# A table for the order of three PSUM banks, and a quarter of one product moved from GpSimd to VectorE

## What is computed

```
dA  = exp(dt[..., None] * A)                       # 256 inner channels x 16 states
dBx = dt[..., None] * B_t[:, None, :] * x_t[..., None]
h   = dA * h + dBx                                 # along the sequence
y   = einsum('bdn,bn->bd', h, C_t)
```

## Time and profile before

| | us |
|---|---|
| median of 3 runs (14129.7 to 14130.83) | 14129.91 |
| the profiled execution | 14134.33 |
| its span, first to last instruction | 14132.5 |

### The profile page before, as it was taken

How to read it: one execution, slowest core, us unless ns; L and a number is a source line. 1 busy time by engine, 2 the same in 40 slices (tenths; PEclk the granted TensorE clock), 3 DMA queues, 4 the chain that set the end, 5 groups by cost and what they waited for, 6 DMA issues and landing times.

```text
span 14132.5 us, 159372 instructions
## 1 busy us (share of the span) xinstructions
PE 11209.6 (79%) x32512; PEld 3280.3 (23%) x32512; DVE 13252.0 (94%) x11827; ACT 12050.3 (85%) x24489; POOL 13788.4 (98%) x3076
## 2 busy tenths in 40 slices
PE   6787777777787878778777778787787878887787
PEld 2222222222222222222222222222222222222221
DVE  7999999999999999999999999999999999999998
ACT  7888888888888888888888888888888888888887
POOL 7999999999999999999999999999999999999999
PEclk8888888888888888888888888888888888888887
DMA  5656565555656565656566565656565665656564
GB/s 131 143 137 143 140 149 138 143 137 145 143 142 145 135 146 140 146 138 142 139 147 144 139 145 136 149 139 143 140 141 142 145 144 137 143 140 149 138 143 113
DMA packets 1068201, 1991.56 MB, mean 141 GB/s; under 512 B 123650, under 2 KB 124731, under 8 KB 1067067
## 3 DMA queue, kind: packets, MB, share of 16 engines
q1 hardware_dynamic: 1065786, 1979.41, 58.8%
q10 hardware_dynamic: 1280, 0.02, 0.0%
HBM read 1626.62 MB, written 352.32 MB: 140 GB/s over the span
## 4 chain that ended last, share of the span: by engine, by line
POOL 66%; issue 31%; DVE 1%; ACT 1%; PE 1%; POOLq 0%; ACTq 0%; DMA 0%; DVEq 0%; SPq 0%
POOL hq L953 50%; POOL dbx L945 16%; DVE hq L844 0%; POOLq L952 0%; ACTq L496 0%; PE pp L378 0%; ACT ps_a L584 0%; PE pp L355 0%; POOLq L944 0%; ACT L544 0%; PE pp L356 0%; PE pp L319 0%; DVE dbx L830 0%; ACT xh L544 0%; POOLq L942 0%
## 5 line engine op out<-in xcount | busy, mean ns | idle before, releaser
L844 DVE TENSOR_TENSOR_SCAN hq<-ps_a,dbx 128x512 f32<-128x512 f32 x8192 | 9507.5, 1208 | 700.1 <-ACT dbx L595 461.5
L953 POOL TENSOR_TENSOR hq<-hq,c_rep 128x2048 f32<-128x2048 f32 x2048 | 9255.2, 4546 | 231.8 <-ACT carry L600 231.3
L584 ACT ACTIVATE ps_a<-dt_rep,A_neg 128x512 f32<-128x512 f32 x8192 | 5621.4, 687 | 1508.4 <-DVE hq L844 1477.7
L945 POOL TENSOR_TENSOR dbx<-dtx_rep,b_rep 128x2048 f32<-128x2048 f32 x1024 | 4646.5, 4538 | 90.9 <-DMA dtx_rep<-dtx_d 90.9
L411 PE MATMUL ps_acc<-hq,dsum 128*32 128x512 f32 x16384 | 2470.3, 679 | 485.8 <-POOL hq L953 482.5
L595 ACT ACTIVATE dbx<-ps_a,dbx,carry 128x1 f32<-128x1 f32 x7168 | 2510.9, 350 | 252.5 <-POOL dbx L945 150.7
L830 DVE TENSOR_TENSOR dbx<-dtx_rep,ps_b 128x2048 f32<-128x2048 f32 x1024 | 2316.7, 2262 | 4.8 <-DMA dtx_rep<-dtx_d 4.8
L319 PE MATMUL pp<-xin,diag 128*128 128x504 f32 (+3 forms) x4608 | 2213.2, 608 | 6.0 <-ACT diag L626 6.0
L399 PE MATMUL ps_b<-dbl,bsel 41*128 41x512 f32 x2048 | 1320.9, 729 | 276.4 <-issue 223.2
L355 PE MATMUL pp<-x,W_taps 128*128 128x512 f32 x768 | 687.2, 993 | 750.1 <-DVE x L804 606.7
L319 PEld LDWEIGHTS pp<-xin,diag 128*128 128x128 f32 x4608 | 792.9, 189 | 1397.9 <-issue 1397.9
(11 more groups left out here) (117 smaller groups left out, 9982.4 us busy)
## 6 DMA issues: line engine op xcount, KB each, us to landing
dtx_rep<-dtx_d SPq DMA_DIRECT2D x2048, 256.0 KB, 4.9
dt_rep<-dt_d SPq DMA_DIRECT2D x2048, 256.0 KB, 5.7
c_rep<-bc_d SPq DMA_DIRECT2D x1024, 256.0 KB, 5.5
b_rep<-bc_d SPq DMA_DIRECT2D x1024, 128.0 KB, 2.9
dtx_d<-sp SPq DMA_DIRECT2D x256, 512.0 KB, 2.8
dt_d<-dt SPq DMA_DIRECT2D x256, 512.0 KB, 6.1
out<-o SPq DMA_DIRECT2D x128, 512.0 KB, 5.2
xin<-in_x SPq DMA_DIRECT2D x192, 320.0 KB, 8.5
```

What stands on the lines that cost most here:

```text
L584: A(ps_a[:, i % RA, :], dt_rep[:, q // NQ, g, :], ACT.Exp, scale=A_neg[:, q // NQ, q % NQ, g:g + 1]).then_inc(exp_done, 1)
L844: v.tensor_tensor_scan(hq[:, q % HQ, g, :], ps_a[:, i % RA, :], dbx[:, slot(q), g, :], 0.0, ALU.mult, ALU.add).then_inc(scan_done, 1)
L945: g.tensor_tensor(dbx[:, slot(q), :, :], dtx_rep[:, d, :, :], b_rep[:, c % 2, q % NQ // 2, :].unsqueeze(1).to_broadcast([P, DG, T]), ALU.m ...
L953: g.tensor_tensor(quad, quad, c_rep[:, c % 2, q % NQ, :].unsqueeze(1).to_broadcast([P, DG, T]), ALU.mult).then_inc(cmul_done, 1)
```

## The change

The bank of a tile comes from a table `BANK`, and the distance to the tile that had it before from `AGE`. The distance is 3, but 2 for tiles 15 and 31, and 4 for the tiles behind them, 16 and the next chunk's 0. Decay, add_carry and scan read the table. Tile 0 of the product of quad 3 (of 4 tiles) is made by VectorE behind the scan of tile 7; GpSimd makes the other three tiles. TensorE selects B for it in slot 6. So `ps_b` is used five times a chunk rather than four, the semaphore `bmul_dve` counts five products, and whoever reads quad 3 waits for both engines.

```diff
--- before.py
+++ after.py
@@ -67,10 +67,16 @@
     return u // 8, 2 * (u % 2) + i % 2, (u % 8) // 2
 
 
-def bank_age(i):
-
-    return RA if i >= RA else next(NT + i - j for j in range(NT - 1, 0, -1) if j % RA == i % RA)
-
+HURRIED = (15, 31)
+BANK = [0, 1, 2]
+for tile in range(3, NT):
+    BANK.append(BANK[tile - (2 if tile in HURRIED else 4 if tile - 1 in HURRIED else 3)])
+AGE = [2 if tile in HURRIED else 4 if (tile - 1) % NT in HURRIED else 3 for tile in range(NT)]
+assert all(BANK[tile] == BANK[tile - AGE[tile]] for tile in range(NT))
+
+BY_DVE = (0, 2, 3, 4, 6)
+ND, SHARED, SPLIT = len(BY_DVE), 3, 1
+PE_SHARED, DVE_SHARED = 6, 7
 
 POOL_CHUNKS, POOL_SLOTS, ATT_CHUNK = (1, 2, 3, 4), (10, 11), CH - 3
 ATT_FC, ATT_H, ATT_MM, ATT_SUM, ATT_EXP, ATT_WTS = 24, 25, 26, 28, 29, 31
@@ -249,7 +255,7 @@
                     sp_e.wait_ge(dtx_out, 16 * (b * CH + c + 1))
                     sp_e.sem_inc(wait_taken, 1)
                 if not (isinstance(b, int) and b * CH + c == 0):
-                    sp_e.wait_ge(bmul_dve, (b * CH + c - 1) * (QUADS // 2) + 2 * (d + 1))
+                    sp_e.wait_ge(bmul_dve, (b * CH + c - 1) * ND + sum(q // NQ <= d for q in BY_DVE))
                     sp_e.sem_inc(wait_taken, 1)
                     sp_e.wait_ge(bmul_pool, (b * CH + c - 1) * (QUADS // 2) + 2 * (d + 1))
                     sp_e.sem_inc(wait_taken, 1)
@@ -392,7 +398,7 @@
                 mm(pp[:, 1, 0:2], w["gblock"][:], gst[:], start=True, stop=True).then_inc(gmm_done, 1)
 
             def select_b(b, c, q):
-                n = (b * CH + c) * (QUADS // 2) + q // 2
+                n = (b * CH + c) * ND + BY_DVE.index(q)
                 pe.wait_ge(dbl_done, b * CH + c + 1)
                 if not (isinstance(n, int) and n == 0):
                     pe.wait_ge(bmul_dve, n)
@@ -420,6 +426,8 @@
                             select_b(b, c, s + 2)
                         elif c + 1 < end:
                             select_b(b, c + 1, 0)
+                    if u == PE_SHARED:
+                        select_b(b, c, SHARED)
                     if c + 1 < end:
                         for d in range(DI):
                             if u == PE_XH[d]:
@@ -547,7 +555,7 @@
                 act.wait_ge(dbl_mm, b * CH + c + 1)
                 if not (isinstance(b, int) and b * CH + c < 2):
                     act.wait_ge(bc_out, 16 * (b * CH + c - 1))
-                    act.wait_ge(bsel_mm, (b * CH + c - 1) * (QUADS // 2))
+                    act.wait_ge(bsel_mm, (b * CH + c - 1) * ND)
                 A(dbl[0:NDBL, c % 2, :], pp[0:NDBL, 0, :], ACT.Copy).then_inc(dbl_done, 1)
 
             def softplus_tail(b, c, k):
@@ -580,19 +588,22 @@
                 if i % (DG * NQ) == 0:
                     act.wait_ge(dt_repd[q // NQ], 16 * NJ * (b * CH + c + 1))
                 if not (isinstance(n, int) and n < RA):
-                    act.wait_ge(scan_done, n - bank_age(i) + 1)
-                A(ps_a[:, i % RA, :], dt_rep[:, q // NQ, g, :], ACT.Exp,
+                    act.wait_ge(scan_done, n - AGE[i] + 1)
+                A(ps_a[:, BANK[i], :], dt_rep[:, q // NQ, g, :], ACT.Exp,
                   scale=A_neg[:, q // NQ, q % NQ, g:g + 1]).then_inc(exp_done, 1)
 
             def add_carry(b, c, i):
                 q, g = divmod(i, DG)
                 m = (b * CH + c) * QUADS + q
                 if g == 0:
-                    act.wait_ge(bmul_pool if q % 2 else bmul_dve, (b * CH + c) * (QUADS // 2) + q // 2 + 1)
+                    if q % 2:
+                        act.wait_ge(bmul_pool, (b * CH + c) * (QUADS // 2) + q // 2 + 1)
+                    if q in BY_DVE:
+                        act.wait_ge(bmul_dve, (b * CH + c) * ND + BY_DVE.index(q) + 1)
                     act.wait_ge(carry_done, m - QUADS + 1)
                 act.wait_ge(exp_done, (b * CH + c) * NT + i + 1)
                 first = dbx[:, slot(q), g, 0:1]
-                A(first, ps_a[:, i % RA, 0:1], ACT.Identity, scale=carry[:, q, g:g + 1], bias=first).then_inc(first_done, 1)
+                A(first, ps_a[:, BANK[i], 0:1], ACT.Identity, scale=carry[:, q, g:g + 1], bias=first).then_inc(first_done, 1)
 
             def keep_carry(b, c, q):
                 n = (b * CH + c) * QUADS + q
@@ -821,27 +832,33 @@
 
             def weigh_inputs(b, c, q):
                 d = q // NQ
-                dve.wait_ge(bsel_mm, (b * CH + c) * (QUADS // 2) + q // 2 + 1)
+                dve.wait_ge(bsel_mm, (b * CH + c) * ND + BY_DVE.index(q) + 1)
                 if q % NQ == 0:
                     dve.wait_ge(dtx_repd[d], 16 * NJ * (b * CH + c + 1))
                 n = (b * CH + c) * QUADS + q
-                if not (isinstance(n, int) and n < 2):
-                    dve.wait_ge(scan_done, DG * (n - 1))
-                v.tensor_tensor(dbx[:, slot(q), :, :], dtx_rep[:, d, :, :],
-                                ps_b[:].unsqueeze(1).to_broadcast([P, DG, T]), ALU.mult).then_inc(bmul_dve, 1)
+                if not (isinstance(n, int) and n < 4):
+                    dve.wait_ge(scan_done, DG * (n - (3 if q == SHARED else 1)))
+                elif n == 2:
+                    dve.wait_ge(scan_done, DG)
+                m = SPLIT if q == SHARED else DG
+                v.tensor_tensor(dbx[:, slot(q), 0:m, :], dtx_rep[:, d, 0:m, :],
+                                ps_b[:].unsqueeze(1).to_broadcast([P, m, T]), ALU.mult).then_inc(bmul_dve, 1)
 
             def scan(b, c, i):
                 q, g = divmod(i, DG)
                 m = (b * CH + c) * QUADS + q
                 if g == 0:
-                    dve.wait_ge(bmul_pool if q % 2 else bmul_dve, (b * CH + c) * (QUADS // 2) + q // 2 + 1)
+                    if q % 2:
+                        dve.wait_ge(bmul_pool, (b * CH + c) * (QUADS // 2) + q // 2 + 1)
+                    if q in BY_DVE:
+                        dve.wait_ge(bmul_dve, (b * CH + c) * ND + BY_DVE.index(q) + 1)
                     if not (isinstance(m, int) and m < HQ):
                         dve.wait_ge(sum_done, m - HQ + 1)
                 if c % CH:
                     dve.wait_ge(first_done, ((b + c // CH) * (CH - 1) + c % CH - 1) * NT + i + 1)
                 else:
                     dve.wait_ge(exp_done, (b * CH + c) * NT + i + 1)
-                v.tensor_tensor_scan(hq[:, q % HQ, g, :], ps_a[:, i % RA, :], dbx[:, slot(q), g, :],
+                v.tensor_tensor_scan(hq[:, q % HQ, g, :], ps_a[:, BANK[i], :], dbx[:, slot(q), g, :],
                                      0.0, ALU.mult, ALU.add).then_inc(scan_done, 1)
 
             def group_stats(b):
@@ -872,6 +889,8 @@
                 for u in range(NT):
                     s, g = divmod(u, DG)
                     scan(b, c, u)
+                    if u == DVE_SHARED:
+                        weigh_inputs(b, c, SHARED)
                     if g == 1 and s % 2:
                         if s + 1 < QUADS:
                             weigh_inputs(b, c, s + 1)
@@ -942,8 +961,9 @@
                     pool.wait_ge(dtx_repd[d], 16 * NJ * (b * CH + c + 1))
                 if not (isinstance(n, int) and n < 4):
                     pool.wait_ge(scan_done, DG * (n - 3))
-                g.tensor_tensor(dbx[:, slot(q), :, :], dtx_rep[:, d, :, :],
-                                b_rep[:, c % 2, q % NQ // 2, :].unsqueeze(1).to_broadcast([P, DG, T]),
+                m = SPLIT if q == SHARED else 0
+                g.tensor_tensor(dbx[:, slot(q), m:, :], dtx_rep[:, d, m:, :],
+                                b_rep[:, c % 2, q % NQ // 2, :].unsqueeze(1).to_broadcast([P, DG - m, T]),
                                 ALU.mult).then_inc(bmul_pool, 1)
 
             def weigh_states(b, c, q):
```

## The result

| | before | after |
|---|---|---|
| median of 9 runs, us | 14130.83 | 14090.08 |
| runs from, to, us | 14128.15 to 14137.01 | 14088.04 to 14091.18 |
| span of the profiled execution, us | 14132.5 | 14089.0 |
| GpSimd busy | 98% | 96% |

The ratio is 0.997, with a 95% interval of 0.9961 to 0.9979. The change is worth 41 us, where 54 were forecast. That is more than the 28 us that a measurement here can tell from no change, and not much more.

The account below looks back on a forecast made before the run. GpSimd bounds three or four chunks of eight by small amounts, a VectorE, ScalarE and TensorE loop hardly shorter. Gains of about 9 us less costs of about 7.3 gave -1.75 a batch, -54 in all: 14,077, range 13,990 to 14,155.

Parts of the forecast that it names:

- GpSimd's saving: GpSimd's quad 3 product covers three tiles rather than four: 1.1 us less, leaving GpSimd 52.7 us per chunk.
- The selection ahead of softplus: TensorE's new selection, between z and dt, delays softplus by 1.05 us in chunk 7, 0.57 in chunk 4; 5.7 over seven chunks.
- cover holds: Rival, chance 0.15: something before softplus shortens as much as TensorE's selection adds; batch falls about 6.3 us, time 13,935.
- Bank order, chunk end: Next tile 0's decay waits for scan 28, not 30: 1.25 us gained at five of eight chunk ends, 0.3 behind 5.
- waits on GpSimd: Stops at tiles 28 and 29 go as GpSimd's products come earlier: 0.3 + 0.2 us in chunks 3 and 4.
- Bank order, middle: Tile 15's decay waits for scan 13, not 12, a microsecond later in chunk 7; ScalarE idles there anyway, so no cost.
- GpSimd's ring: Rival, chance 0.28: GpSimd's state product, carry and input product loop closes at 52.7 us; a quarter microsecond more means 14,130.
- dt rows late: Slower rival, chance 0.1: dt_rep transfers land 1.4 us later, delaying tile 0's decay; +4.75 us a batch, 14,277 in full.
- Chunk 5, "about 0": Forecast change in chunk 5's length: about 0, with only about 0.3 us gained behind it because attention fills the place.
- Chunk 8, "cost 1.6 us": Tile 31's decay, ahead of rstd and the silus, waits for scan 29, moving chunk 8's tail 1.6 us per batch.
- The 4.13 us of issue at the loop's end follow as before: At the loop's end, behind chunk 8's later tail, the issue time was taken as unchanged at 4.13 us.
- Chunk 1, -0.2: Forecast change in chunk 1's length: 0.2 us shorter per batch.

Follow-up runs that it names:

- conv_behind_dt: The kernel after, with the first two convolution taps moved from slots 8 and 9 to behind the dt product of slot 10; 14055.87 us, ratio 0.9943 against before.
- select_before_z: The kernel after, with the fifth selection in TensorE's slot 5, ahead of the second z product; 14090.32 us, ratio 0.9966 against before.
- product_only: The kernel after, with VectorE's small product and its selection but the old order of banks; 14253.51 us, ratio 1.0085 against before.
- the store runs: The kernel after with rstd ahead of tile 31's decay in chunk 8, 14083.79 us; the same storing 64 of each 1024 output columns, 14058.45 us.

## Why the prediction was right, and where not

**GpSimd's saving: right.** 1.1 us was taken, 1.08 measured. The estimate from the Trainium skill (GPSIMD Engine Reference, Performance versus the Vector engine) was 1.11, and the trace agrees within 0.03. GpSimd's sizes here are 2361, 3448 and 4529 ns for 1024, 1536 and 2048 elements, which leaves about 0.2 us fixed.

**The selection ahead of softplus: right in kind, too small in size.** L809 was to come at 27.5 us, and came at 27.62 to 27.74, and at 28.20 in chunk 1. Over seven chunks that is a charge of 7.0 us, where 5.7 had been taken between two rows, of chunks 4 and 7; chunks 1 and 5 lose more than chunk 4 does. VectorE's wait at the small product (0.78 us) and ScalarE's before Abs in chunks 1 to 4 are where they were named. Doubling the selection and moving the convolution behind dt both moved the time the way this step says, so the rival "cover holds" is out.

**Bank order, chunk end, and waits on GpSimd: right.** 25.1 us behind softplus against 25.06, in all six plain chunks. The gain behind softplus is 8.1 us a batch, against 8.4 in the forecast (9 less 0.6 in chunk 8). What the prediction didn't see is that this gain exists only once GpSimd is relieved: alone the bank order made the kernel slower.

**Bank order, middle: right.** The decay of tile 15 waits 0.99 us for the scan, and 0.83 us of waiting for TensorE still follow, so nothing is lost.

**GpSimd's ring: close, as feared.** It was put at 52.7 us. The kernels that freed TensorE met it: in conv_behind_dt chunk 3 fell into it, in select_before_z tile 4 waits for it.

**dt rows late: did not happen.** No wait stands at tile 0 in chunks 2 to 8.

**Chunk 5, "about 0": the step that failed.** It grew by 1.01 us, 31 us over the kernel. The two parts of the chunk say where. Softplus comes 1.09 us later (26.61 to 27.70), more than the 0.57 to 1.05 that the forecast had for the selection, and behind it the chunk is only 0.08 us shorter (28.92 to 28.84), where the bank order and the waits on GpSimd were to give all of it back. product_only has the selection without the bank order, and its chunk 5 takes 56.44 us: softplus at 27.53, then 28.91. So 0.9 of the 1.01 us are the selection's charge, and it isn't covered there.

From tile 30 to the next tile 0 the bank order does bring its 0.3 us in chunk 5 (4.31 to 4.00), but from softplus to tile 30 0.24 of them go again, and in that stretch stands the attention. VectorE at its last product, and TensorE ahead of it:

```profile
7401.27 0.17 DVE L784 TENSOR_TENSOR att<-pp,w_spke_b 128x13 f32<-128x13 f32 x1 [1.28 <-PE pp L314]
```

```profile
7396.04 0.22 PE L309 MATMUL pp<-part,w_fc_wT 128*16 128x8 f32 x2 [1.54 <-ACT sq L583]
...
7398.34 1.94 PE L417 MATMUL ps_acc<-hq,dsum 128*32 128x512 f32 x8
7400.20 0.58 PE L313 MATMUL pp<-hrep,w_ch_wT 16*128 16x2 f32 x2
7400.65 0.58 PE L314 MATMUL pp<-w_spke_wT,hrep 16*128 16x13 f32 x2
```

The windows of 10.5 us that end where VectorE takes that product, in the kernel before and after:

```profile
7412.59:7423.09 10.50, 8.31 (x29) 2.28 (x25) 9.94 (x11) 10.18 (x24) 10.50 (x3) 0.67 0.82 192
```

```profile
7390.77:7401.27 10.50, 7.09 (x21) 2.18 (x20) 8.95 (x10) 10.10 (x26) 10.50 (x3) 0.70 0.85 195
```

VectorE's wait for TensorE there grew from 22.8 to 43.4 us over all 32 batches. TensorE idles 1.54 us ahead of the first attention product, against 0.96 on average before; over the whole window the granted clock is about the same, and from the first attention product to VectorE's it is 0.50 after and 0.56 before, on average. That wait is not the 1.01 us: in product_only it is 0.92 us a batch against 0.51 before, and what follows softplus lasts as long as before. Why it grew stays open. I said that attention fills the place of the gain, and never asked what then covers the charge.

**Chunk 8, "cost 1.6 us": mis-sized.** The tail did move, by 1.36 us. ScalarE and VectorE in chunk 8 of after:

```profile
7563.56 0.69 ACT L592 ACTIVATE ps_a<-dt_rep,A_neg 128x512 f32<-128x512 f32 x1 [1.62 <-DVE hq L861]
```

```profile
7567.65 2.23 DVE L886 TENSOR_TENSOR o<-pp,x 128x512 f32<-128x512 f32 x3 [1.94 <-ACT pp L624]
...
7577.93 1.22 DVE L861 TENSOR_TENSOR_SCAN hq<-ps_a,dbx 128x512 f32<-128x512 f32 x1 [2.49 <-ACT dbx L606]
```

But "The 4.13 us of issue at the loop's end follow as before" was wrong: from branch to instruction it is 3.66 us after and 4.90 before, so 1.24 of the 1.36 came back, and the chunk changed by -0.07. I had treated the loop's end as a fixed price; the store runs show that part of it is waiting for something else that was under way.

**Chunk 1, -0.2:** it was +0.27, with a wait of 1.3 us at its small product, against 0.8 to 1.2 in the other plain chunks; its softplus comes 1.51 us later than before. So the forecast was near because an undercharge of 1.3 us a batch at softplus (chunks 1 and 5 above all) met an overcharge of 1.1 in chunk 8. Direction, mechanism and the level of plain chunks were right; that the miss is only 13 us is partly luck.

## What to carry to other kernels

Here the fullest engine and the loop of the others were about 2% apart, each half of the change alone lost, and both together won: in such a case relieve both in one change, and test the halves. Where a stage "fills the place" of a gain, ask what covers the costs there; here nothing did. Price a fixed gap at a loop's end by what it waits for, and not by its length before. Where VectorE and GpSimd work side by side, keep one input of VectorE's operations in PSUM, even if TensorE must put it there.

## What the hardware showed that was not expected

- VectorE's 512-element product with both inputs in SBUF took 5.5 us on average beside a busy GpSimd; 99 of 256 waited for three GpSimd operations, like the row of 10.12 us, and the other 157 for one. With one input in PSUM it takes 0.69 us.
- TensorE's granted clock read 0.67 in the 10.5 us that follow a pause of 1.62 us, and 1.00 around the same products a chunk later, behind one of 1.02; the dbl product took 3.64 us in the one and 1.91 in the other. In the kernel before, a pause of 1.59 us left the clock at 1.00.
- A repeat of the same selection costs TensorE 0.86 us and the first 1.05.
- The time from a loop's branch to the next pass's first instruction on VectorE was 3.66 to 4.90 us, and 2.93 with fifteen sixteenths of the output stores left out.
